# Front loads on one queue in the order of need, and three moves around them, in a cross-attention and FFN kernel

## What is computed

```python
def layernorm(x): return (x - mean(x)) / sqrt(var(x) + 1e-5)

q = layernorm(x) @ Wq                      # 256 -> 512
k, v = context @ Wk, context @ Wv          # 192 -> 512
attn = softmax(q @ k.T * 64 ** -0.5)       # per head, over 77 columns
x = x + (attn @ v) @ Wo + bo

r = layernorm(x)
h = layernorm(r) * gamma + beta
w1 = (fc1_q - 128) * fc1_scales            # groups of 128 rows
w2 = (fc2_q - 128) * fc2_scales
x = x + r + 0.5 * (silu(h @ w1 + b1) @ w2 + b2)
```

## Time and profile before

| | |
|---|---|
| median of 3 runs | 187.17 us (186.95 to 187.19) |
| the profiled execution | 187.28 us, its span 185.5 us |
| busy in the span | PE 179.3 (97%), DVE 122.4, ACT 122.7, GpSimd 115.6 us |
| chain that ended last | PE 89%, DMA 4%, ACT 2%, DVE 2% |
| granted clock of TensorE | 1.00 in every slice |

### The profile page before, as it was taken

The page is one execution under the profiler, slowest core; times in us unless marked ns, Lnnn a source line. Parts: engine busy times, 40 slices in busy tenths (PEclk is TensorE's granted clock), DMA queues, the critical chain, the costliest instruction groups (busy, mean ns, idle before and its releaser), DMA issues.

```text
span 185.5 us, 3896 instructions
## 1 busy us (share of the span) xinstructions
PE 179.3 (97%) x1502; PEld 175.3 (95%) x1502; DVE 122.4 (66%) x262; ACT 122.7 (66%) x230; POOL 115.6 (62%) x159
## 2 busy tenths in 40 slices
PE   7789999999999999999999999999999999999994
PEld 7579889899999999999999999999999999999993
DVE  1179987999987474946496459846694768164341
ACT  3268771797968960898188935895389717952580
POOL 5021997697968974298809971598449763766220
PEclk9999999999999999999999999999999999999999
DMA  5997891000001000010001000100001000100101
GB/s 168 330 379 199 271 402 65 2 2 0 4 0 58 4 0 0 4 57 0 4 0 57 4 0 0 61 2 0 0 16 44 0 4 0 60 0 0 57 4 57
DMA packets 8904, 10.72 MB, mean 58 GB/s; under 512 B 2332, under 2 KB 6455, under 8 KB 8759
## 3 DMA queue, kind: packets, MB, share of 16 engines
q1 hardware_dynamic: 8421, 9.96, 16.1%
q10 hardware_dynamic: 466, 0.53, 0.9%
HBM read 8.38 MB, written 2.10 MB: 57 GB/s over the span
## 4 chain that ended last, share of the span: by engine, by line
PE 89%; DMA 4%; ACT 2%; DVE 2%; ACTq 1%; POOL 0%; issue 0%
PE H L902 24%; PE T L916 22%; PE T L884 15%; PE S L863 15%; PE S L870 4%; DMA wv_b<-in_L_xattn_Wv 4%; PE S L813 4%; PE T L846 2%; PE S L832 1%; PE H L832 1%; PE H L846 1%; ACT L388 1%; DVE pT_lo L628 0%; PE T L797 0%; ACT m_hi L414 0%; ACT pT_hi L442 0%
## 5 line engine op out<-in xcount | busy, mean ns | idle before, releaser
L322 POOL TENSOR_TENSOR y_lo<-y,y_hi 128x512 fp32r<-128x512 f32 x28 | 37.8, 1368 | 2.4 <-ACT y_hi L469 2.0
L902 PE MATMUL H<-hT_hi,w_hi 128*128 128x256 f32 x128 | 36.8, 287 | 0.0
L916 PE MATMUL T<-w_hi,y_hi 128*128 128x256 f32 x128 | 36.5, 285 | 0.0
L288 POOL TENSOR_TENSOR probs<-probs,rsum 128x616 f32<-128x616 f32 x16 | 19.2, 1219 | 27.1 <-DVE rsum L623 27.1
L902 PE MATMUL H<-hT_lo,w_hi 128*128 128x256 f32 x128 | 35.4, 277 | 0.0
L916 PE MATMUL T<-w_lo,y_hi 128*128 128x256 f32 x128 | 35.4, 277 | 0.0
L902 PE MATMUL H<-hT_hi,w_lo 128*128 128x256 f32 x128 | 35.4, 277 | 0.0
L916 PE MATMUL T<-w_hi,y_lo 128*128 128x256 f32 x128 | 35.4, 276 | 0.0
L465 ACT ACTIVATE y<-H,vec 128x256 f32<-128x256 f32 x64 | 26.6, 469 | 6.6 <-PE H L902 6.6
L438 ACT ACTIVATE probs<-probs,rstd 128x616 f32<-128x616 f32 x16 | 12.8, 808 | 22.7 <-DVE probs L611 22.6
L628 DVE TENSOR_TENSOR pT_lo<-S,pT_hi 128x640 fp32r<-128x640 f32 x16 | 13.2, 822 | 18.3 <-ACT pT_hi L442 18.3
(11 more groups left out here) (138 smaller groups left out, 458.9 us busy)
## 6 DMA issues: line engine op xcount, KB each, us to landing
q_sb<-in_L_ffn_fc_q SPq DMA_DIRECT2D x2, 1024.0 KB, 8.0
out_x<-x_sb SPq DMA_DIRECT2D x16, 128.0 KB, 1.8
x_sb<-in_x SPq DMA_DIRECT2D x7, 256.0 KB, 8.0
s_sb<-in_L_ffn_fc_scales SPq DMA_DIRECT2D x2, 512.0 KB, 11.2
s_sb<-in_L_ffn_fc_scales SPq DMA_DIRECT2D x1, 1024.0 KB, 7.8
wq_sb<-in_L_xattn_Wq SPq DMA_DIRECT2D x1, 512.0 KB, 4.2
wo_sb<-in_L_xattn_Wo SPq DMA_DIRECT2D x1, 512.0 KB, 7.5
wk_a<-in_L_xattn_Wk SPq DMA_DIRECT2D x1, 256.0 KB, 2.7
```

Source lines behind the costliest of these rows:

```text
L288: nc.gpsimd.tensor_tensor(p, p, rsum[:, j, :].unsqueeze(2).to_broadcast([P, HEADS, J]), ALU.mult).then_inc(norm_done, 1)
L322: nc.gpsimd.tensor_tensor(y_lo[:, two, :], y[:, two, :], f32(y_hi[:, two, :]), ALU.subtract).then_inc(y_lo_done, 1)
L902: ins = mm(r[:, q * W:(q + 1) * W], wt[:, c, m * P:(m + 1) * P], ht[:, c, :], start=c == q == i == 0, stop=c == q == 1 and i == 2)
L916: ins = mm(o, yt[:, m, j * P:(j + 1) * P], wt[:, m, :], start=m == 0 and i == 0, stop=m == M - 1 and i == 2)
```

## The change

It makes four edits in the head of the kernel. No arithmetic is changed.

- The five transfers that ACT issued at its start are issued by SP: wk_b's halves behind wk_a, wv_b's halves behind wv_a, x's pair 0 behind these and ahead of wo.
- PE computes V ahead of pair 0's transposes; ACT places V ahead of `x_hi(0)`; DVE places V ahead of `stats1(0)` and `x_lo(0)`.
- The two warming products behind the context's transposes are gone.
- On GpSimd `rsqrt1(1)` moves from ahead of w1's dequantization to between pair 0's two `root2`, and `lower_w1(2)` from ahead of these to behind the wait for both `hn` tiles of pair 0.

```diff
--- before.py
+++ after.py
@@ -228,8 +228,13 @@
             def _(sp):
                 sp.dma_start(ctx_sb[:, :, :], ctx_v).then_inc(ctx_in_sem, 16)
                 sp.dma_start(wk_a[:, :], wk[0:P, :]).then_inc(wk_in, 16)
+                for g in range(2):
+                    sp.dma_start(wk_b[g * DH:(g + 1) * DH, :], wk[P:DC, g * INNER // 2:(g + 1) * INNER // 2]).then_inc(wk_b_in, 16)
                 sp.dma_start(wq_sb[:, :, :], wq.rearrange("(n p) f -> p n f", p=P)).then_inc(wq_in, 16)
                 sp.dma_start(wv_a[:, :], wv[0:P, :]).then_inc(wv_in, 16)
+                for g in range(2):
+                    sp.dma_start(wv_b[g * DH:(g + 1) * DH, :], wv[P:DC, g * INNER // 2:(g + 1) * INNER // 2]).then_inc(wv_b_in, 16)
+                sp.dma_start(x_sb[:, pair(0), :], x_v[:, 0, :, :]).then_inc(x_in[0], 16)
                 sp.dma_start(wo_sb[:, :, :], wo.rearrange("(n p) f -> p n f", p=P)).then_inc(wo_in, 16)
                 sp.dma_start(x_sb[:, pair(1), :], x_v[:, 1, :, :]).then_inc(x_in[1], 16)
                 sp.dma_start(q1_sb[:, :, :], q1.rearrange("(n p) f -> p n f", p=P)).then_inc(q1_in, 16)
@@ -332,7 +337,6 @@
                     nc.gpsimd.tensor_tensor(w1_lo[:, c, cols], w1_sb[:, c, cols], f32(w1_hi[:, c, cols]), ALU.subtract).then_inc(w1_split, 1)
 
                 rsqrt1(0)
-                rsqrt1(1)
                 pool.wait_ge(s1_in[0], 16)
                 dequantize_w1(0)
                 dequantize_w1(1)
@@ -343,11 +347,12 @@
                 lower_w1(0)
                 lower_w1(1)
                 dequantize_w1(3)
+                root2(0, 0)
+                rsqrt1(1)
+                root2(0, 1)
+
+                pool.wait_ge(hn_done, UT)
                 lower_w1(2)
-                root2(0, 0)
-                root2(0, 1)
-
-                pool.wait_ge(hn_done, UT)
                 lower_w1(3)
                 residual_roots(0)
                 normalize(1, 0)
@@ -386,11 +391,6 @@
             def _(act):
                 act.wait_ge(half_ready, 1)
                 nc.scalar.activation(table_probe[:, 0:1], neg_half[:, 0:1], ACT.Exp)
-                for g in range(2):
-                    act.dma_start(wk_b[g * DH:(g + 1) * DH, :], wk[P:DC, g * INNER // 2:(g + 1) * INNER // 2]).then_inc(wk_b_in, 16)
-                act.dma_start(x_sb[:, pair(0), :], x_v[:, 0, :, :]).then_inc(x_in[0], 16)
-                for g in range(2):
-                    act.dma_start(wv_b[g * DH:(g + 1) * DH, :], wv[P:DC, g * INNER // 2:(g + 1) * INNER // 2]).then_inc(wv_b_in, 16)
 
                 def place_k(n):
                     name = f"K{n}"
@@ -489,10 +489,10 @@
                 place_k(1)
                 center_wq(0)
                 center_wq(1)
-                x_hi(0)
                 act.wait_ge(vT_zeroed, 1)
                 place_v(0)
                 place_v(1)
+                x_hi(0)
                 for n in range(4):
                     m_hi_part(0, n)
                 act.wait_ge(bo_in, 16)
@@ -682,11 +682,11 @@
                 nc.vector.tensor_copy(ctxT_b[DH:P, :], r[DH:P, 0:BJ]).then_inc(freed["S0"], 1)
                 sum_wq(0)
                 sum_wq(1)
-                stats1(0)
                 dve.wait_ge(vT_zeroed, 1)
-                x_lo(0)
                 place_v(0)
                 place_v(1)
+                stats1(0)
+                x_lo(0)
                 for n in range(4):
                     m_lo_part(0, n)
                 dve.wait_ge(bo_hi_done, 1)
@@ -926,14 +926,13 @@
                     for b in range(B):
                         ins = nc.tensor.transpose(r[0:last - first, b * J:(b + 1) * J], ctx_sb[:, b, first:last], ident[0:J, 0:J])
                     fill(f"ctxT{n}", ins)
-                warm(2)
                 wait_freed(pe, "ctxT0")
                 project("K", wk_in, wk_b_in, wk_a, wk_b)
                 pe.wait_ge(wq_in, 16)
                 transpose_wq(0)
                 transpose_wq(1)
+                project("V", wv_in, wv_b_in, wv_a, wv_b)
                 x_transposes(0)
-                project("V", wv_in, wv_b_in, wv_a, wv_b)
                 for name in ("K0", "K1", "WQ0", "WQ1"):
                     wait_freed(pe, name)
                 for c in range(C):
```

More of the change, by code:

```diff
@@ L345, in _ @@
                 dequantize_w1(3)
-                lower_w1(2)
                 root2(0, 0)
+                rsqrt1(1)
                 root2(0, 1)
                 pool.wait_ge(hn_done, UT)
+                lower_w1(2)
                 lower_w1(3)
```

## The result

| | before | changed |
|---|---|---|
| median (lowest to highest), us | 187.18 (186.89 to 187.72), 6 runs | 185.90 (185.62 to 186.41), 6 runs |
| span of the profiled execution | 185.5 | 183.8 |
| that execution's own time | 187.28 | 185.62 |

The medians are 1.3 us apart, 0.7%. The estimated ratio of the times, which goes by all executions and not by the medians, is 0.9928, with a 95% interval of 0.9913 to 0.9943. The profiled execution is the quickest of its six, so its trace shows 1.7 us of gain where the medians show 1.3.

What follows compares the result with a forecast made beforehand. PE was taken as the bound, with three transfer holes in its head and DVE setting the pace behind M. A gain of 2.3 less 0.2 gave 2.1, so 185.1 us; own range 184.8 to 185.6, eight in ten 184.6 to 186.2.

Steps and rivals of the forecast that it cites:

- my own case: Whole kernel: the steps hold as summed, 185.1 us, range 184.8 to 185.6; chance 0.72.
- B: Head transfers: bubbles bring V or x's pair 0 0.4 to 1.2 us late, 185.5 to 186.4; chance 0.13.
- C: Middle: late s1 or DVE and GpSimd crowding delays a normalization 1 to 2 us, 186.2 to 187.2; chance 0.05.
- the 0.2 that I took off for pair 1: GpSimd, second normalization: the extra lower_w1 makes it 0.1 to 0.3 us late, taken as 0.2.
- K's first half: PE's head: without the two warming products it starts at 4.63 for 4.89 and ends at 5.72.
- Wq: PE's head: wq lands by 6.2, so its transposes start at 6.44 without a wait and end at 7.30.
- the queue doesn't run dry: SP's queue: x's pair 0, the ninth transfer, is issued near 4.6 with 1.4 MB still queued ahead.
- V and x's transposes: PE's head: V's second half from 8.39 to 8.89, then x's transposes until 9.27.
- DVE takes the bound: DVE before the scores: m_lo ends at 13.4 to 13.6, PE waits some 0.3, gain 2.3 us, not PE's 2.83.
- GpSimd ahead of pair 0: GpSimd: dequantizations start near 15.1, end near 18.9, before normalization at 20.1; cover of 1.1 us, no gain by itself.
- rival D: PE's head: without warm-up PE works at 1.2 GHz, costing some 4 us, ending near 189; chance 0.02.
- Rival A: Head transfers: landings follow issue, wv_b lands at 11.8 again; 1.2 to 1.3 us slower, 188.5; chance 0.03.

Runs made afterwards that it cites:

- pool_back: The changed kernel with GpSimd's `rsqrt1(1)` and `lower_w1(2)` back in their old places: median 185.68 us, ratio 0.9910 to the kernel before.
- warm_back: The changed kernel with the two warming products behind the context's transposes put back: median 186.28 us, ratio 0.9958 to the kernel before.
- q_only: The kernel before with only the transfers' new order and issuer: median 186.37 us, ratio 0.9946.
- v_only: The kernel before with only V moved ahead of x's transposes, statistics and x_lo, transfers as before: median 187.92 us, ratio 1.0033.
- no_first_warm: The changed kernel without the six warming products (twelve loads) at the start: median 187.07 us, ratio 0.9986 to the kernel before.
- experiment 5: The changed kernel with `warm(2)` put back behind the context's transposes: median 186.28 us, ratio 0.9958 to the kernel before.

## Why the prediction came out as it did

The forecast was 185.1, the result 185.9: right in sign and in the main mechanism, and inside the range of 184.6 to 186.2. It lies outside my own case's range of 184.8 to 185.6, in the part that rivals B and C had added, and small forms of both occurred. The gain was over-estimated, 2.1 for 1.3. Part of the nearness is luck: the 0.2 that I took off for pair 1 did not come, and offset part of what I had missed.

*K's first half, right:* 4.56 for 4.63 forecast, and its second half at 5.81 for 5.72. Both hold for an execution with the quick pace.

*Wq, wrong by 0.3.* I had wq landing at 6.2 at the latest and Wq's transposes at 6.44; they started at 6.73, behind a wait of 0.36. I counted the bytes ahead of wq and divided by a rate. But SP issued it only at 2.83, behind two issues of 0.6 for wk_b, where I had taken 0.48 an issue, and the engines were nearly idle from 4.5 to 5.0 (share 0.31, 68 GB/s). The claim that "the queue doesn't run dry" was the step that failed. The Trainium skill, "DMA: Bandwidth & Descriptors", section "Anatomy of one DMA — SWDGE (gpsimd) path", states a fixed cost of about 2 us for one transfer whatever its size; it is told there for transfers that GpSimd issues, and most of it is put behind the last byte. Here the rate picks up at 5.0, 2.2 us behind the start of wq's issue from SP; that is of the same size but lies ahead of the bytes, so the page does not explain it.

*V and x's transposes:* 8.90 and 9.62 for 8.39 and 8.89. Besides wq's 0.3 there are the gaps of 0.16 at each wait; the earlier trace rows shows one, and I did not count the others. M started at 10.21 for 9.55, right behind x's transposes: the wait of 0.3 for wqT, which was centered by 9.78, did not come.

*DVE takes the bound, right.* The last m_lo ended at 13.85 (forecast 13.4 to 13.6) and PE waited 0.33 (0.3). Because DVE bound, only part of PE's lateness came through: x's second transposes gained 2.00, for 2.3.

*GpSimd ahead of pair 0, wrong by 0.4.* I had the dequantization starting near 15.1 and 1.1 us of cover. s1 came at 17.1, past my own sign for rival C (16.3), and the cover was gone. I had written that s1's bytes ahead are the same, "so they land as before"; before, GpSimd began at 18.59 and nothing in its rows showed when s1 had landed. It was a bound from above that I used as a value. The price can be read on PE's side: PE's gap ahead of pair 0's probability transposes is 0.65 for 0.26.

*Normalization of pair 1, wrong by 0.2 to the other side.* It was not late: the roots took 1.87 us (33.76 to 35.63) for 2.27, and it waited 0.35 for its sums. In its place came the slower cast of h, 0.27, which was given back before the next pair.

*The sum* in the profiled executions is then 2.3 - 0.3 - 0.4 = 1.6 where the span gained 1.7 (185.5 to 183.8).

*From there to the medians, 0.4 more.* The two profiled executions are 1.66 us apart, the medians 1.28. Of that, 0.10 is the profiled execution before, which lay above its median. My rival D spoke of the slow pace as all or nothing, and gave it 0.02. What the runs show is a third thing, which I had not listed: the moment of the step differs between executions of one code, and before the change its effect ended in the 1.36 us in which PE waited for wk_b anyway. With that hole closed K's second half stands at 5.81 or at 6.53 in the same kernel, and at 6.82 in pool_back. The execution with 6.53 took 185.83 where that with 5.81 took 185.62, so a late step can carry some 0.2 of the rest. How many of the unprofiled executions had one isn't known, so this last term is argued and not shown. A forecast from one profiled execution had no means to show this, but the earlier trace rows held the hint: loads 0.21 apart until about 4, in a head that I was about to strip of its holes.

*Which part brought what.* The order of the transfers alone gives 0.8 of the 1.3. V ahead and the removed warming give the other 0.5 together; V ahead without the transfers costs 0.7, and in warm_back, where wv_b was late by 0.80, V ahead shows no advantage over q_only (186.28 and 186.37). The warming's share is then most of that 0.5 by the medians, but the intervals don't settle the split. GpSimd's part gives nothing.

Rival A's mechanism is shown by v_only, at 0.7 where I priced 1.2 to 1.3, and did not occur in the change since wv_b came in time. B is what happened with wq, whose 0.3 is the larger part of the 0.5 by which V's second half came late, and, in warm_back, with wv_b. C happened at 0.4, not at 1 to 2.

## What to carry to other kernels

Before counting a closed hole as gain, ask what else ended inside it: here a varying start-up of PE and a late s1 were both covered by one wait for a transfer, and both came to light when it was gone. When transfers are put into one queue, lay out the issue times too; a 64 KB piece took SP as long to issue as a large one, and with two of them ahead of a large one the engines moved 25 to 146 GB/s from 3.5 to 5.0. A consumer's start is only an upper bound of its transfer's landing, and no value to move others against.

## What the runs showed of the hardware that I had not expected

**PE's pace has a step whose moment varies.** Loads of the first warming stand 0.21 us apart, those of K's first half 0.12 to 0.14 when quick and about 0.26 when slow (0.56 and 1.02 for four). In the changed kernel the step lies near 4.0 in one execution, and within K's first half, near 6, in another; over the kernels of the study with the first warming it lies between 4.0 and some 6.7, and without the first warming it came only near 9. The granted clock in the profile reads 0.999 or 1.00, that is the level of 2.4 GHz, in all these stretches, also in those at half pace, so durations show the step and that column does not. The Trainium skill, "TensorE: Matmul & The Clock Gate", Part 1, says that the array is throttled until activity releases it; the order of events agrees (no_first_warm), the column doesn't show it. What sets the moment within one code stays open, and so does whether the two removed products bring it forward (experiment 5).

**Small transfers.** Each piece of wk_b (two of 64 KB) lands 2.6 to 2.8 us behind its issue in the changed kernel, with only ctx and wk_a ahead in the queue, and both are there only at 7.34 and 7.46 beside a 512 KB transfer of another queue. The two issues took SP 1.19 us.

**DVE beside GpSimd.** The cast of 128x256 took 0.56 to 0.58 us in the eight profiles in which GpSimd's subtraction of 128x512 reached into it, and 0.28 in the six in which GpSimd was past that and ran only operations on 128x2.

**Late issues wait.** SP's transfer of the bias row, issued at 14.59 while the large loads were queued, held SP for 3.38 us; before the change, at 16.53, it took 0.58. It cost nothing here, since its reader is the attention output at 24.5.
